# A graph-attention layer on one core: a new order of its steps, and the second FFN product as three f32r products

## The reference

```python
q, k, v = h @ Wq, h @ Wk, h @ Wv            # 8 heads of 64
e = einsum('ehd,ehd->eh', k[src], q[dst]) / sqrt(64)
ex = exp(e - segment_max(e, dst)[dst])       # softmax over the edges of one dst
attn = ex / segment_sum(ex, dst)[dst]
a = segment_sum(attn[:, :, None] * v[src], dst)
x1 = layernorm(h + a @ Wo, ln1_g, ln1_b)
f = relu(x1 @ W1 + b1) @ W2 + b2             # 512 -> 64 -> 512
y = layernorm(x1 + f, ln2_g, ln2_b)
out = layernorm(x + y)
```

## Time and profile before

| | us |
|---|---|
| median of 3 runs | 682.72 (682.36 to 683.36) |
| span of the profiled execution | 682.0 |
| TensorE busy | 641.5 (94%) |
| DVE busy | 578.0 (85%) |
| ACT busy | 528.3 (77%) |
| GpSimd busy | 401.7 (59%) |

### The profile page before, as it was taken

The page is one execution under the profiler, slowest core; times in us unless marked ns, Lnnn a source line. Parts: engine busy times, 40 slices in busy tenths (PEclk is TensorE's granted clock), DMA queues, the critical chain, the costliest instruction groups (busy, mean ns, idle before and its releaser), DMA issues. The chain is left out here.

```text
span 682.0 us, 10864 instructions
## 1 busy us (share of the span) xinstructions
PE 641.5 (94%) x3520; PEld 483.8 (71%) x3520; DVE 578.0 (85%) x1391; ACT 528.3 (77%) x1140; POOL 401.7 (59%) x363
## 2 busy tenths in 40 slices
PE   5999999999999999999999999999999999999950
PEld 2778877777777777777777777777778778675520
DVE  7668769879898898898889889988989898899792
ACT  2525269877888987988798889878878999698881
POOL 7267244867675865756776574864547726735423
PEclk9999999999999999999999999999999999999995
DMA  7844154644643745674474456455554824536452
GB/s 227 220 101 133 44 123 106 173 122 142 148 121 131 159 121 148 167 157 92 146 177 117 113 161 137 105 168 123 127 128 155 184 62 135 139 77 138 131 113 91
DMA packets 37747, 91.44 MB, mean 134 GB/s; under 512 B 8346, under 2 KB 9642, under 8 KB 37690
## 3 DMA queue, kind: packets, MB, share of 16 engines
q0 software_dynamic: 31536, 82.74, 47.6%
q1 hardware_dynamic: 6154, 8.01, 4.3%
HBM read 71.20 MB, written 20.99 MB: 135 GB/s over the span
## 5 line engine op out<-in xcount | busy, mean ns | idle before, releaser
L558 ACT ACTIVATE squares<-rows,nmean 125x512 bf16<-125x512 f32 x200 | 142.3, 713 | 41.5 <-DVE nmean L902 19.8
L412 POOL DMA_INDIRECT x_rows<-in_x_dram,node_idx x40 | 48.2, 1205 | 56.8 <-DVE rows L917 47.3
L416 POOL DMA_INDIRECT out_dram<-rows,node_idx x40 | 46.4, 1160 | 56.4 <-ACT rows L618 47.0
L473 POOL DMA_DIRECT2D x_rows<-in_L_gnn_ln_b_dram x40 | 52.9, 1372 | 31.1 <-DVE rows L821 21.7
L898 DVE SCALAR_TENSOR_TENSOR rows<-pF,rows 125x512 f32<-125x512 f32 x78 | 50.6, 686 | 23.2 <-PE pF L1103 22.5
L963 PE MATMUL pP<-wo_hi,aT_hi 128*125 128x512 f32 x160 | 65.9, 412 | 0.3 <-DVE aT_lo L848 0.3
L963 PE MATMUL pP<-xTs_hi,wv_hi 128*128 128x500 f32 x160 | 65.8, 411 | 0.0
L963 PE MATMUL pP<-xTd_hi,wq_hi 128*128 128x500 f32 x160 | 65.4, 409 | 0.1
L963 PE MATMUL pP<-xTs_hi,wk_hi 128*128 128x500 f32 x160 | 63.5, 397 | 0.6 <-ACT q L539 0.6
L963 PE MATMUL pP<-wo_lo,aT_hi 128*125 128x512 f32 x160 | 63.1, 394 | 0.0
L963 PE MATMUL pP<-wo_hi,aT_lo 128*125 128x512 f32 x160 | 63.0, 394 | 0.0
(11 more groups left out here) (197 smaller groups left out, 1760.6 us busy)
## 6 DMA issues: line engine op xcount, KB each, us to landing
x_rows<-in_L_gnn_ln_b_dram POOLq DMA_DIRECT2D x40, 512.0 KB, 6.7
dst_row<-in_dst_dram SPq DMA_DIRECT2D x9, 250.5 KB
q<-in_L_gnn_Wq_dram SPq DMA_DIRECT2D x1, 1024.0 KB, 5.6
rows<-in_L_gnn_Wk_dram SPq DMA_DIRECT2D x1, 1024.0 KB, 7.8
rows<-in_L_gnn_Wv_dram SPq DMA_DIRECT2D x1, 1024.0 KB, 6.8
x_rows<-in_L_gnn_Wo_dram SPq DMA_DIRECT2D x8, 128.0 KB, 6.0
xd<-in_x_dram,dst_idx POOLq DMA_INDIRECT x40, 4.6
xs<-in_x_dram,src_idx POOLq DMA_INDIRECT x40, 3.8
```

The source lines that it names most:

```text
L412: pool.indirect_dma_start(rows, None, x, bass.IndirectOffsetOnAxis(ap=table[:, column:column + 1].bitcast(U32), axis=0), bounds_check=N - ...
L416: pool.indirect_dma_start(out, bass.IndirectOffsetOnAxis(ap=table[:, column:column + 1].bitcast(U32), axis=0), rows, None, bounds_check=N ...
L473: pool.dma_start(xr_wide[n], bass.AP(tensor=be2.tensor, offset=be2.offset, ap=[[0, P], [0, 2], [1, D]]), accum_op=ALU.add).then_inc(s[f"be ...
L558: ins = act.activation(squares[:, t, :], w[n][:, t, :], ACT.Square, bias=nmean[c][n][:, t:t + 1], accum_out=sq[c][n][:, t:t + 1])
```

## The change

- **PLAN** has a due time of its own for each of the ten rounds and every step. The fillers are 23, all in round 0; there are none at the end.
- **F2** becomes three f32r products on each half: hT and W2 are split into high and low parts. W2's parts are made once (FHI on ACT, FLO on DVE). For hT there is a new step, lo, on DVE in each job, between ReLU and the second bias copy, which becomes a step of its own (seed1) and waits for lo. b1 is put into the bank before F1 instead of in ReLU.
- **Gathers first**: dst_idx is copied as soon as dst is transposed (TABD). GpSimd gathers the dst rows ahead of its iotas and other set-up (INIT). W_k is fetched behind the dst gathers, W_v behind the src gathers.
- **Tile-wise turning**: TXD and TXS take one tile with its four chunks each, so a step waits only for its own tile's gather.
- dst_row loses its own tile and shares weight's; it is fetched after log_taken instead of after mask_eq. Only two jobs are closed in the other way (E0 and E1 of the last round).
- Between a round's two table loads ACT has no Sqrt step.

```diff
@@ PE, F2
-                        for t in range(2):
-                            pe.matmul(pF[1 - t][0:R, :], hT[DFF * t:DFF * t + DFF, :], w2[DFF * t:DFF * t + DFF, :],
-                                      start=False, stop=True, skip_group_check=True).then_inc(s["f_filled"], 1)
+                        on.wait_ge("w2_lo", 1)
+                        on.wait_ge("h_lo", nth("dve.lo", slot, i))
+                        for a, b in ((0, 0), (1, 0), (0, 1)):
+                            for t in range(2):
+                                half = slice(DFF * t, DFF * t + DFF)
+                                ins = pe.matmul(f_banks(i, slot)[t][0:R, :], hT[a][half, :], w2[b][half, :],
+                                                start=False, stop=(b == 1), skip_group_check=True)
+                                if b == 1:
+                                    ins.then_inc(s["f_filled"], 1)
@@ ACT, F1 and the bias copy
-                        act.activation(hT[:, :], pF[0][:, 0:R], ACT.Relu, bias=b1_col[:, :]).then_inc(s["h_done"], 1)
-                        on.wait_ge("h_done", nth("act.F1", slot, i))
-                        act.activation(pF[0][0:R, :], bias_all[0:R, :], ACT.Copy).then_inc(s["seeded_1"], 1)
+                        act.activation(hT[0][:, :], hidden(i, slot), ACT.Relu).then_inc(s["h_done"], 1)
+                    elif what == "seed1":
+                        on.wait_ge("h_lo", nth("dve.lo", slot, i))
+                        act.activation(pF[0][0:R, :], bias_all[0:R, :], ACT.Copy).then_inc(s["seeded_1"], 1)
@@ DVE, new step
+                    elif what == "lo":
+                        on.wait_ge("h_done", nth("act.F1", slot, i))
+                        dve.scalar_tensor_tensor(hT[1][:, :], hidden(i, slot), 0.0, hT[0][:, :].bitcast(F32), ALU.max, ALU.subtract)\
+                            .then_inc(s["h_lo"], 1)
@@ DVE, tables
-                elif step == "TABS":
+                elif step == "TABD":
                     on.wait_ge("tables_clear", 5)
                     on.wait_ge("idx_turned", 1)
+                    dve.tensor_copy(dst_idx[0:R, :], pF[0][0:R, 0:CT]).then_inc(s["tables_done"], 1)
+                elif step == "TABS":
@@ PE, turning
-                    on.wait_ge(f"{which}_loaded", 64 * (i + 1))
+                    on.wait_ge(f"{which}_loaded_{t}", 16 * (i + 1))
                     bank_free(i, step)
-                    for t in range(4):
-                        ins = pe.transpose(pT_of(i, step)[:, R * t:R * t + R], rows[0:R, t, P * k:P * k + P], ident[0:R, 0:R])
+                    for k in range(KC):
+                        ins = pe.transpose(pT_of(i, step)[:, R * k:R * k + R], rows[0:R, t, P * k:P * k + P], ident[0:R, 0:R])
@@ SP
-            sp.dma_start(stage["k"], Wk.rearrange("(k p) n -> p k n", p=P)).then_inc(s["wk_loaded"], 16)
...
+            for t in range(4):
+                on.wait_ge(f"xd_loaded_{t}", 16)
+            for h in range(2):
+                sp.dma_start(stage["2"][DFF * h:DFF * h + DFF, :], W2).then_inc(s["w2_loaded"], 16)
+            sp.dma_start(stage["k"], Wk.rearrange("(k p) n -> p k n", p=P)).then_inc(s["wk_loaded"], 16)
@@ PLAN, two of some hundred lines
+TURN1 271; TURN2 506; OFFS 604; TURNF 710; TXD0 900 3149 7219 15246 21583 24405 32373 39246 43912 51372; TXD1 1051
+GXD 420 1923 5155 10335 15461 22535 26266 32901 40037 46200; INIT 1024; GXS 1319 2672 7476 12561 17710 24023 30253
+FILLERS = {(0, "TURN1"): 7, (0, "OFFS"): 2, (0, "TURNF"): 4, (0, "TXD0"): 3, (0, "TXD1"): 3, (0, "TXD3"): 4}
```

407 lines of the change are left out of this document (212 added, 195 removed).

## The result

| us | before | after |
|---|---|---|
| median | 682.84 (682.36 to 683.36, 4 runs) | **699.94** (696.06 to 701.15, 4 runs) |
| span of the profiled execution | 682.0 | 699.0 |
| first K product of round 0 | 35.6 | 35.6 |
| first K product of the last round | 567.5 | 575.7 |
| from there to the end | 114.5 | 123.3 |

The changed kernel is slower: 1.0239 times the time before, interval 1.0211 to 1.0268. The forecast was 673.2, in a range from 668 to 682. The profiled execution took 700.75 us.

The account below looks back on a forecast made before the run. TensorE's queue was taken to set the pace from first Q to last-round K, with start and tail apart. 682.0 - 4.6 (start) - 5.4 (F2) + 0.5 (hand-over) + 0 (tail) = 672.5, plus 0.7 gives 673.2 us; range 668.0 to 682.0.

Parts of the forecast that it names:

- The second FFN product: F2 in each job: six f32r products pair up, saving 0.17 us a job, 5.4 us by the last round's K.
- Rivals 2 and 3: F2: half-height f32r products don't pair up (696, chance 0.06); F2's weight loads don't hide (679, chance 0.08).
- I take +0.5 us over the whole run and keep 0 to 12: Between F1 and F2: cost of DVE's low-half step and its hand-over, +0.5 us, bounds 0 to 12.
- Rival 1: F2 waits for DVE's low half in many jobs, stalling TensorE 0.3 us x 40: 684.7 us, chance 0.14.
- a cover of 1.7: Between bias copy and F2: 1.7 us of slack, in which DVE's 0.3 plus a 0.2 hand-over fits.
- The new order: Rounds' step order: most F2 stand two or more products behind F1, against one; no cost of its own in the sum.
- The start: Up to Q0: earlier gathers move it from 20.98 to about 15.8 us; -4.6 us in all, bounds -2 and -6.
- The lower bound of -2: Start: gain only 2 us if the first gather goes at 5.9 or TensorE begins its products at lower clock.
- The tail: From the last round's first K: freed fillers and one more job's work cancel; 0, between -4 and +6 us.
- rival 4: Tail: TensorE's clock falls without fillers, 3 us on the last job's chain: 676 us, chance 0.08.
- Sqrt and the tables: ACT: as many table loads in both orders and no Sqrt between a round's two loads; worth 0.
- ten or more: Sign in the waits list: that many microsecond TensorE waits on hT's low half or bias copy mean the hand-over stalls TensorE.

Follow-up runs that it names:

- f2_one_pair: Changed kernel in its own order, but F2 as before (one f32 product a half, no VectorE step or hand-over): 702.0 us, ratio 1.0283.
- f2_only: Kernel before with only F2 as three f32r products, low part and bias copy behind ReLU, destination row fetched into the far tile: 697.3 us, ratio 1.0219.
- f2_par: Kernel before with only three-product F2; ReLU writes to SBUF, ScalarE copies the bias at once, VectorE makes both parts: 689.6 us, ratio 1.0084.
- fi_gaps: Changed kernel with destination row fetched into the far tile and FI steps of rounds 4 to 9 placed where GpSimd was free: 693.6 us, ratio 1.0160.
- start_only: Kernel before with only the changed start and turning by tiles; old order, end and F2: 682.26 us, ratio 0.9989.
- mid_one_pair: Changed kernel's start and end, with before's order between the two K products and F2 as before: 695.2 us, ratio 1.0182.
- tail_fill: Changed kernel with 84 fillers (products nothing reads) at five waits of the last 75 us: 697.8 us, ratio 1.0219.
- iota_first: Kernel before with only the changed start, but GpSimd's long iota ahead of the gathers again: 682.05 us, ratio 0.9988.
- old_end: Changed kernel up to the last round's first K, then before's order with its three closing jobs and fillers: 705.4 us, ratio 1.0322.
- row_in_far: Changed kernel with the destination row of rounds 1 to 9 fetched into the far tile instead of the weights' tile: 700.05 us, ratio 1.0214.
- fi_spread: Changed kernel with the FI steps of rounds 4 to 9 moved behind the mask step of their own round: 711.5 us, ratio 1.0400.

## Why the prediction was wrong, point by point

- **The second FFN product** was right: it pairs up, its weight loads hide, and it saves 0.16 us a job (forecast 0.17). Rivals 2 and 3 have fallen.
- **"I take +0.5 us over the whole run and keep 0 to 12"** for the hand-over is the first failed term. In the changed order it cost some 4 us (f2_one_pair). There F2's own waits are 1.1 us in the middle and 6.1 behind it. In before's order it put 10.7 us of idle time into the middle (f2_only), 0.33 us for each of 32 jobs, and 5.6 us behind it; f2_par took 7.7 us of that back. Rival 1 had the mechanism, and its 0.3 us a job is the size in before's middle, though it was written for the changed order, where F2's waits are few. The failed step is "a cover of 1.7": I held one instruction's length against the distance, when the chain had gone from one queue to three, of which VectorE's is busy 87% of the middle.
- **The new order** had no cost in my sum. This is the larger failure. With the old product the changed kernel takes 702.0, 19 us more than before (f2_one_pair). I had taken the middle as bound by TensorE's queue in either order, because in the order before it was. I looked at what F2's distance became, and not at the distances of gathers, scatters and index transfers. For the row of destinations I wrote "some 6 us of other steps in front of the next mask, 0": the fetch is issued at 295.3 us and VectorE waits 3.28 us for it, then TensorE 2.52. The FI steps, ten of them now in rounds 0 to 2, I did not speak of; they delayed a gather so that VectorE waited 3.02 us for it. Without both the kernel is 5.4 to 6.4 us shorter (fi_gaps). The rest of the 19 us is spread over waits that were not taken apart, so the step that failed is shown and its causes only in part.
- **The start** gained 1.7 to 2.3 us of the 4.6 (start_only, mid_one_pair). At 35.6 us the first K product is where it was, with two turning steps and FOLD already done. The first gather went at 4.47, not 3.6; VectorE lost 1.9 us beside the iota; and TensorE began its products at half clock, from 16.7 to 20.1 us. The lower bound of -2 names the last of these.
- **The tail, "0, between -4 and +6"**: +8.8. Its direction was open in the text and its mechanism was not rival 4: with the clock held up the stretch is 0.5 us shorter. Freed fillers were worth nothing, since TensorE is not what this stretch waits for: 84 fillers put in leave it as long as it was (tail_fill).
- **Sqrt and the tables, turning by tiles**: 0 as said. Both traces have 21 table loads, and start_only has the tile-wise turning in all rounds with 2.2 us idle in the middle.
- Of what would show it, the test for rival 1 ("ten or more") counted only the waits of one kind. After has four of F2 on the bias copy, 5.6 us, and is still 17 us slower.

What stays open: of the changed kernel's middle, 693.6 is reached by removing two causes, and the rest (11.3 us idle, with the scatter of slot E0 as its largest single place) is not taken apart; and how the 8.8 us of the end divide between order, hand-over and lateness.

## What to carry to other kernels

When one engine is full and the others wait for it, an order written by hand hides the transfers' and the other queues' times behind it, and a new order must be costed by those distances: for each gather, scatter and fetch, when it is issued, how long it took in the trace, and when it is needed. A shorter instruction on the full engine is worth its saving only if no new hand-over stands in front of it; count queues crossed, not the length of the added instruction. If a hand-over can't be avoided, take other work (here the bias copy) out of its series.

## What was not expected of the hardware

- **An iota on GpSimd holds up some VectorE instructions for its whole length.** In four traces (before, after, start_only, iota_first) the VectorE step beside the 1.95 us iota took 1.5 to 2.6 us: a cast in before (1.72) and in iota_first (1.53), where two such casts together take 0.34 in after, away from the iota; a tensor_scalar in after (2.37) and start_only (2.62), where it takes 0.44 to 0.50 in the other two. All read one f32 or int32 tile from SBUF. In after the step's record begins 0.4 us ahead of the iota's and ends with it. A cast out of PSUM beside the iota in iota_first (3.31 us) took 0.20. The Trainium skill, "SBUF — State Buffer", section "SBUF: two separate sides", says that VectorE in a two-port mode and GpSimd take a shared pair of ports for a whole instruction, the other being blocked. These rows agree with the blocking. In which mode the steps ran no row says, and the page gives the pair to whichever starts first, while VectorE's record began first here.
- **A TensorE wait of 2 to 3 us is often followed by 3.4 us at half clock, and not always.** In the changed kernel this was so at 170, 309 and 462 us (waits of 2.68, 2.52 and 2.14), in tail_fill at 269 and 460 (2.41 and 3.49). But the 1.89 us at 404 in the changed kernel, the 2.00 at 395 in fi_gaps and even the 3.43 us at 171 in old_end had full clock behind them. The waits of 1.3 us in f2_only had none behind them either: its granted clock is at full from 12 us to 623 us. So the length of the wait alone does not tell what the clock will do.
- **Repairs of single stalls did not add up one by one**: 0 (row_in_far) and +11.6 us (fi_spread), but -6.4 together with FI in GpSimd's free places, which also differ from fi_spread's. And the changed kernel's runs spread over 5 us, row_in_far's over 9, those of before beside them over 1 us. The fetch of the row of destinations took 7.4 us from issue to landing in after and 5.6 at the same place in tail_fill: with stops that depend on when a transfer lands, the time is less steady.
